# The end of a softmax attention core: the last batch's context and output product go to two free PSUM banks, and the last two batches' row numbers are worked out on VectorE

## The reference

```python
x = x + 0.5 * ffn_block(layernorm(x))
x = x + linear_attention(layernorm(x))
x = x + 0.5 * ffn_block(layernorm(x))

def ffn_block(x):
    h = layernorm(x, ln1_scale, ln1_shift)
    x = x + softmax_attention(h)            # 16 heads of 8, causal; ctx @ wo + bo
    h = layernorm(x, ln2_scale, ln2_shift)
    return x + moe(h)                       # 8 experts, the best 2 by h @ gate_w
```

## Time and profile before

| what | value |
|---|---|
| time, median of 3 runs | 1330.87 us (1326.74 to 1331.21) |
| the profiled execution's own time | 1331.67 us |
| its span, first to last instruction | 1329.9 us |
| mean granted TensorE clock | 0.890 of full speed |
| busy share PE / DVE / ACT / POOL | 76% / 81% / 58% / 41% |
| scatters to `xs` (L1385) | 128, busy 166.8 us in all |
| `back_rstd`, first instruction (L1411) | 32, mean 1373 ns, 232 to 1560 ns |

### The profile page before, as it was taken

How to read it: one execution, slowest core, us unless ns; L and a number is a source line. 1 busy time by engine, 2 the same in 40 slices (tenths; PEclk the granted TensorE clock), 3 DMA queues, 4 the chain that set the end, 5 groups by cost and what they waited for, 6 DMA issues and landing times.

```text
span 1329.9 us, 33572 instructions
## 1 busy us (share of the span) xinstructions
PE 1012.5 (76%) x11497; PEld 753.1 (57%) x11644; DVE 1077.7 (81%) x2383; ACT 771.4 (58%) x1170; POOL 549.9 (41%) x787
## 2 busy tenths in 40 slices
PE   2789888888826998367788858998898888369980
PEld 1567666666624666245455546676676666246660
DVE  5889999999965887687588768899999998458875
ACT  1369787777724555133555534687777787245550
POOL 3402456555663666210033240034465456536660
PEclk9889999999957999566888879999999999579995
DMA  3574233225202332233222206111111010023326
GB/s 101 180 233 126 83 114 112 92 78 159 62 19 73 90 89 65 89 118 116 69 64 65 62 3 202 55 40 36 40 48 44 28 50 18 21 72 88 89 65 197
DMA packets 146339, 111.57 MB, mean 84 GB/s; under 512 B 15664, under 2 KB 140848, under 8 KB 146224
## 3 DMA queue, kind: packets, MB, share of 16 engines
q1 hardware_dynamic: 124080, 78.70, 20.4%
q0 software_dynamic: 9088, 18.76, 4.0%
q10 hardware_dynamic: 13056, 12.59, 2.7%
HBM read 43.49 MB, written 59.82 MB: 78 GB/s over the span
## 4 chain that ended last, share of the span: by engine, by line
DVE 36%; issue 21%; PE 18%; ACT 11%; POOL 8%; DMA 3%; DVEq 1%; ACTq 1%; SPq 1%; POOLq 0%
DVE negm L1031 7%; POOL ys L1434 4%; DVE negm L1035 3%; DVE p_lo L1274 3%; PE banks L422 2%; ACT pf L848 2%; DVE pf L1281 2%; DVE p_lo L1043 2%; DVE x_all L989 2%; ACT p_hi L718 2%; PE banks L457 2%; PE banks L437 1%; ACT yb L741 1%; PE banks L444 1%; DVE p_lo L1047 1%
## 5 line engine op out<-in xcount | busy, mean ns | idle before, releaser
L701 ACT ACTIVATE pf<-banks 128x1536 f32<-128x1536 f32 x128 | 185.8, 1451 | 112.8 <-PE banks L444 110.0
L1043 DVE TENSOR_TENSOR p_lo<-pf,p_hi 128x1536 f16<-128x1536 f32 x128 | 223.9, 1750 | 2.9 <-ACT p_hi L718 1.9
L1434 POOL DMA_INDIRECT ys<-y_out,dest x156 | 151.6, 972 | 115.8 <-ACT y_out L854 90.8
L718 ACT CAST p_hi<-pf 128x1536 f16<-128x1536 f32 x128 | 188.7, 1474 | 2.0
L1385 POOL DMA_INDIRECT xs<-n_all,slot x128 | 166.8, 1303 | 54.9 <-issue 37.6
L1411 POOL TENSOR_SCALAR rs<-mv 128x2 f32<-128x2 f32 x32 | 43.9, 1373 | 334.3 <-DVE mv L1096 278.1
L1031 DVE TENSOR_REDUCE negm<-banks 128x4 f16<-128x1024 f32 x128 | 156.0, 1219 | 18.2 <-PE banks L422 8.9
L444 PEld LDWEIGHTS banks<-ident,negm 128*128 128x128 f16 x1536 | 122.1, 100 | 82.6 <-issue 10.0
L437 PE MATMUL banks<-qst,kst 96*128 96x512 f16 x384 | 151.5, 395 | 2.5 <-ACT pf L701 2.5
L444 PE MATMUL banks<-ident,negm 128*128 128x128 f16 x1536 | 153.1, 223 | 0.3 <-issue 0.2
L422 PE MATMUL banks<-kst,qst 96*128 96x128 f16 x1536 | 129.8, 221 | 30.6 <-DVE negm L1031 20.2
(11 more groups left out here) (197 smaller groups left out, 2471.0 us busy)
## 6 DMA issues: line engine op xcount, KB each, us to landing
xs<-zeros SPq DMA_DIRECT2D x128, 130.0 KB
qk_d<-p_hi ACTq DMA_DIRECT2D x48, 256.0 KB, 2.2
x_nats<-xs SPq DMA_DIRECT2D x78, 130.0 KB
qst<-qk_d SPq DMA_DIRECT2D x192, 48.0 KB
kst<-qk_d SPq DMA_DIRECT2D x48, 192.0 KB
pf<-ys SPq DMA_DIRECT2D x32, 256.0 KB, 3.1
v_hl<-v_all SPq DMA_DIRECT2D x48, 136.0 KB
qk_d<-p_lo SPq DMA_DIRECT2D x96, 64.0 KB, 1.7
```

The source lines that it names most:

```text
L701: nc.scalar.activation(pf[:, g % 2, :, :, :].rearrange(flat), banks_t[:, :, :].rearrange("p a b -> p (a b)"), ACT.Exp, scale=HD ** -0.5).t ...
L718: nc.scalar.copy(p_hi[:, g % 2, :, :, :].rearrange(flat), pf[:, g % 2, :, :, :].rearrange(flat))\
L1043: nc.vector.tensor_tensor(lo, pf[:, g % 2, :, :, :].rearrange(flat), hi, ALU.subtract)\
L1434: nc.gpsimd.indirect_dma_start(ys, bass.IndirectOffsetOnAxis(ap=dest[:, t % YB, h:h + 1], axis=0), y_out[:, t % YB, h, :], None).then_inc( ...
```

## The change

It rearranges the code behind the loop in the two softmax cores, for batches 14 and 15.

- Batch 15's context turn and output product no longer use `mx`. They go to `psum[0]` and `psum[1]`, two of the three banks of natural scores, whose last use is the scores of batch 15's last group. A semaphore `last_ctx` orders the four steps (`last_turn`, `last_turned`, `last_wo`, `back_add`). The bias is put in ahead, in `last_bias`.
- The order of the uses of `mx` is then: rank of 13, h2, gate and rank of 14, h2, gate and rank of 15.
- PE: `last_turn` stands before `back_h2` of 14, `last_wo` before its `back_gate`.
- ACT: `y_hat` and `pv_read` of 15 stand before `n2_norm` of 14, `last_turned` behind it. A wait for `n2_kept` stands before `n2_norm` of 15.
- DVE: the low part of batch 15's last group stands before `place_of` of 13 and `x_step` of 14; `back_add` of 15 before `choose` of 14.
- The row numbers of batches 14 and 15 are made on DVE (a new `slots` there), right behind `place_of`. POOL makes them for the batches up to 13.
- POOL: the last scatter of batch 12 stands before `back_rstd` of 14, and `back_rstd` of 15 before the last scatter of 13.
- `split_low(2)` moves behind the tables of the first expert stage.

```diff
         def fill_no(ph, b, name):
...
-            if name == "rank" and isinstance(b, int) and b == B - 1:
-                return 5 * b + 4
+            if isinstance(b, int) and b >= B - 2 and name not in ("b1", "b3"):
+                return {(B - 2, "b6"): 0, (B - 2, "b8"): 1, (B - 2, "rank"): 2, (B - 1, "b6"): 3, (B - 1, "b8"): 4,
+                        (B - 1, "rank"): 5}[b, name] + 5 * B - 8
...
+            def last_turn(ph):
+                pe.wait_ge(ph["cx_in"], ph["n"] * B + B)
+                for t in range(T):
+                    ins = nc.tensor.transpose(psum[0][:, t * P:(t + 1) * P], cx[:, t, :], ident[:, :])
+                ins.then_inc(last_ctx, 1)
+            def last_bias():
+                nc.tensor.matmul(psum[1][:, 0:T * P], ident[:, :], bo_b[:, :].unsqueeze(1).to_broadcast([P, T, P]),
+                                 start=True, stop=False, skip_group_check=True)
+            def last_wo(ph):
+                pe.wait_ge(last_ctx, of_last(ph, 2))
+                for t in range(T):
+                    ins = nc.tensor.matmul(psum[1][:, t * P:(t + 1) * P], cxt[:, t * P:(t + 1) * P], w_o[ph["w"]][:, :],
+                                           start=False, stop=True, skip_group_check=True)
+                ins.then_inc(last_ctx, 1)
...
                 if ph["soft"]:
                     back_rank(ph, B - 3)
-                    back_h2(ph, B - 2)
-                    back_gate(ph, B - 2)
+                    last_bias()
...
                 values(ph, B - 1, S - 1, at(0))
-                back_turn(ph, B - 1)
-                back_wo(ph, B - 1)
+                if ph["soft"]:
+                    last_turn(ph)
+                    back_h2(ph, B - 2)
+                    last_wo(ph)
+                    back_gate(ph, B - 2)
...
+            def last_turned(ph):
+                sc.wait_ge(last_ctx, of_last(ph, 1))
+                nc.scalar.copy(cxt[:, :], psum[0][:, 0:T * P]).then_inc(last_ctx, 1)
...
                 p_high(ph, B - 1, S - 1)
                 if ph["soft"]:
+                    y_hat(ph, B - 1)
+                pv_read(ph, B - 1, 1)
+                if ph["soft"]:
                     n2_norm(ph, B - 2)
-                    y_hat(ph, B - 1)
+                    last_turned(ph)
                     h2_turned(ph, B - 2)
                     gates_out(ph, B - 2)
                     keep_n2(ph, B - 2)
-                pv_read(ph, B - 1, 1)
-                ctx_turned(ph, B - 1)
                 if ph["soft"]:
+                    sc.wait_ge(ph["n2_kept"], B - 1)
                     n2_norm(ph, B - 1)
...
+            def slots(ph, b):
+                c = Chain(ve, ph["cp_slot"], b * 5)
+                ve.wait_ge(ph["cp_slot"], 5 * b)
+                c.link(nc.vector.tensor_tensor(at_slot[:, :, :, :], onehot2[:, b, :, :, :],
+                                               pos[:, b, :, :].unsqueeze(2).to_broadcast([P, T, 2, E]), ALU.mult))
+                for w in (4, 2, 1):
+                    c.link(nc.vector.tensor_tensor(at_slot[:, :, :, 0:w], at_slot[:, :, :, 0:w],
+                                                   at_slot[:, :, :, w:2 * w], ALU.add))
+                nc.vector.tensor_copy(slot[:, T * b:T * (b + 1), :], at_slot[:, :, :, 0]).then_inc(ph["cp_slot"], 1)
...
                 back_add(ph, B - 2)
                 if ph["soft"]:
+                    p_low(ph, B - 1, S - 1)
                     place_of(ph, B - 3)
                     x_step(ph, B - 2)
-                    p_low(ph, B - 1, S - 1)
-                    choose(ph, B - 2)
                 back_context(ph, B - 1)
                 if ph is phases[0]:
                     split_low(0)
                 back_add(ph, B - 1)
                 if ph["soft"]:
+                    choose(ph, B - 2)
                     place_of(ph, B - 2)
+                    slots(ph, B - 2)
                     x_step(ph, B - 1)
                     if ph is phases[0]:
                         split_low(1)
                     choose(ph, B - 1)
-                    if ph is phases[0]:
-                        split_low(2)
                     place_of(ph, B - 1)
+                    slots(ph, B - 1)
...
                 tables()
+                if m is mixtures[0]:
+                    split_low(2)
                 full(0)
...
+                    scatter(ph, B - 4, 3)
                     back_rstd(ph, B - 2)
-                    scatter(ph, B - 4, 3)
                     slots(ph, B - 3)
-                    for n in range(4):
+                    for n in range(3):
                         scatter(ph, B - 3, n)
                     back_rstd(ph, B - 1)
-                    slots(ph, B - 2)
+                    scatter(ph, B - 3, 3)
                     for n in range(4):
                         scatter(ph, B - 2, n)
-                    slots(ph, B - 1)
                     for n in range(4):
                         scatter(ph, B - 1, n)
```

More of the change, by code:

```diff
@@ L235, in build @@
                        **sems(n, of_soft if soft else of_linear)) for n, soft in enumerate((True, False, True))]
-        e_in = sem("e_in")
+        e_in, last_ctx = sem("e_in"), sem("last_ctx")
         mixtures = [dict(**sems(f"m{n}", "x_turn x_hi_in h2f_in x_lo_in up_done silu_in hid_in hid_hi_in hid_lo_in down_done "
@@ L265, in at_loop, with of_last @@
             return lambda d: ((4 + n + d) % RB, i + (4 + n + d) // RB)
+        def of_last(ph, n):
+            return ph["n"] // 2 * 4 + n
         def fill_no(ph, b, name):
@@ L544, in attention @@
                 values(ph, B - 1, S - 1, at(0))
-                back_turn(ph, B - 1)
-                back_wo(ph, B - 1)
+                if ph["soft"]:
[3 more added lines that the diff above has]
+                    back_gate(ph, B - 2)
+                else:
+                    back_turn(ph, B - 1)
+                    back_wo(ph, B - 1)
                 if ph["soft"]:
@@ L826, in attention @@
                     keep_n2(ph, B - 2)
-                pv_read(ph, B - 1, 1)
-                ctx_turned(ph, B - 1)
+                else:
+                    ctx_turned(ph, B - 1)
                 if ph["soft"]:
+                    sc.wait_ge(ph["n2_kept"], B - 1)
                     n2_norm(ph, B - 1)
@@ L1068, in back_add @@
             def back_add(ph, b):
-                ve.wait_ge(ph["filled"], fill_no(ph, b, "b3") + 1)
-                src = mx[:, 0:T * P].rearrange("p (t d) -> p t d", t=T)
+                last = ph["soft"] and isinstance(b, int) and b == B - 1
+                if last:
+                    ve.wait_ge(last_ctx, of_last(ph, 3))
+                else:
+                    ve.wait_ge(ph["filled"], fill_no(ph, b, "b3") + 1)
+                src = (psum[1] if last else mx)[:, 0:T * P].rearrange("p (t d) -> p t d", t=T)
                 c = Chain(ve, ph["cv_back"], b * ph["back_links"])
@@ L1089, in back_add @@
                     ve.wait_ge(ph["n2_in"], b)
-                nc.vector.tensor_tensor(y2[:, :, :], src, yb[:, :, :], ALU.add).then_inc(ph["emptied"], 1)
-                ve.wait_ge(ph["emptied"], fill_no(ph, b, "b3") + 1)
+                ins = nc.vector.tensor_tensor(y2[:, :, :], src, yb[:, :, :], ALU.add)
+                if last:
+                    ins.then_inc(last_ctx, 1)
+                    ve.wait_ge(last_ctx, of_last(ph, 4))
+                else:
+                    ins.then_inc(ph["emptied"], 1)
+                    ve.wait_ge(ph["emptied"], fill_no(ph, b, "b3") + 1)
                 for t in range(T):
```

## The result

The changed kernel takes 1308.72 us (median of 6 runs, 1306.4 to 1313.6), the kernel before 1326.78 beside it (6 runs, 1323.56 to 1331.21): a ratio of 0.9864 with an interval of 0.9838 to 0.9889. The forecast was 1315, its range 1309 to 1322: the direction is right, and the time lies 0.3 us under the range. The profiled execution took 1313.6 us, 18.07 less than the one of before (1331.67), with a span of 1311.5.

What follows compares the result with a forecast made beforehand. Each softmax core's last scatter was taken to open the expert stage, so its delay bounds the kernel. 1331.67 - 8.4 (first core) - 7.7 (second) = 1315.6, or 1314.8 from the median; stated as 1315 us, range 1309 to 1322.

Steps and rivals of the forecast that it cites:

- Rival 3: Both ends: batches 14 and 15 still run one after the other; 1329 to 1331 us, no change; chance 0.05.
- rival 2: Both ends: dearer handovers and `slots` at its upper bound, so only part is kept; 1320 us; chance 0.17.
- Rival 4: Expert stages: TensorE's clock stays at 1.2 GHz for longer, cancelling the gain or reaching 1339 us; chance 0.04.
- batch 15's statistics: Both ends: they reach POOL 8.1 us behind the start, at 376.6 in the first core and 1144.1 in the second.
- the third pass: First core, behind the tables: ends at 396.2, costing nothing while the 2.3 us before the first tile last.
- The first weight pass: First core, DVE from 372.5 to 374.8: holds batch 13's first scatter on POOL to 375.65.
- The second weight pass: First core, DVE from 380.45 to 382.75: holds the scatter behind batch 15's root to 383.6.
- signs that the prediction gave for being wrong: Root of 15 waits for something besides POOL's queue, POOL waits for `slot` in the first core, or first tile for DVE.
- the first core's term: First softmax core's end: last scatter issued at 392.85 in place of 401.26, 8.4 us sooner.
- the second's: Second softmax core's end: last scatter issued at 1157.8 in place of 1165.48, 7.7 us sooner.
- the base of the sum: Whole kernel: the profiled execution's 1331.67 us, from which the gains were taken, 0.8 above the median of the runs.
- rival 1: First core: scatters slip past the weight passes, so batch 15's numbers set the end; some 3 us more, 1312; chance 0.14.

Runs made afterwards that it cites:

- passes_moved: The changed kernel with the first weight pass ahead of `back_add` of 14 and the second where the first stood: 1305.44 us, 0.9832 against the kernel before.
- fill_for_passes: The changed kernel with the first two weight passes replaced by fills of zero, leaving out the low parts of `w1` and `w2`: 1304.69 us, one execution.
- slots_pool: The changed kernel with the row numbers of batches 14 and 15 made on POOL again: 1317.1 us, 0.9921 against the kernel before.
- numbers_of_three: `passes_moved` with the first core's row numbers of batch 13 also made on DVE: 1313.7 us, 0.9889 against the kernel before.
- slots_alone: The kernel before with only row numbers of 14 and 15 on DVE, POOL's new order and the third pass behind the tables: 1318.82 us, 0.9927.

## Why the prediction was right, and where not

**What holds.** The last scatter sets each end, its coming sooner is worth its microseconds once per core, and the two ends gave 7.5 and 8.0 us for 8.4 and 7.7. Rival 3 falls: the batches interleave. So does rival 2: `slots` on DVE took from 389.42 to 390.43, 1.0 us for 1.1, and from the end of batch 15's root to its numbers were 7.2 us (383.27 to 390.43), as foreseen (380.0 to 387.2). Rival 4 falls: the two expert stages together took 267.42 us before and 266.77 after, at clocks of 0.95 and 0.96, and 266.6 to 267.7 in the other profiles.

Step by step in the first core, counted from POOL's start: batch 14's root was held by the low part (1.53) as forecast; batch 15's statistics were done 8.1 us behind (377.32), which with the 0.2 us to POOL makes 8.3 for 8.1; the third pass ended at 399.08, 1.0 us before the first tile was in (397.87 + 2.23 = 400.10), where 2.3 were forecast. In the second core the root of 15 began at 8.69 (8.67 foreseen) and the numbers let POOL go on at 17.62 (17.9).

**Terms that were off.** All times from POOL's start at 368.50 or 369.26. *The first weight pass* was to hold the first scatter of 13, to 7.15. It held the cast ahead of it instead (2.12 us), and the scatter after that ended at 7.75. The root behind it on POOL was put off by the same 0.6: it began at 10.35 for 9.7. *The second weight pass* was to hold the scatter behind the root. It came at 11.67 (foreseen 11.95), and the root's last instruction at 11.69 (foreseen 11.3), so it held that: the root was done at 14.0 for 11.5. A scatter held there would have cost POOL's queue alone; a root held there also delays batch 15's normalisation, gate and numbers. So the numbers came at 21.2 for 18.7. POOL's queue was free for them at 20.6, where 20.5 was foreseen, so the numbers came last, and not the queue, which was to be later by 1.8 us. This is one of the signs that the prediction gave for being wrong: in the first core POOL stands waiting for `slot`. The hold could have been read from before, where the second pass, right behind the residual step of 15 as in the changed kernel, held that root's third instruction (2.73); the forecast took the root at its price without a hold and had it done 0.45 us ahead of the pass. `passes_moved` and `fill_for_passes` show what it cost: with the root's instruction back at 0.19 the end loses 1.5 and 3.5 us, the latter with the other hold gone too. Together the first core's term was 0.9 too large, the second's 0.3 too small; the sum of 16.1 compares with 15.6 in the profile. So this wrong step did not carry the time out of the range.

**The step that failed** is the base of the sum and its allowance. It was taken from the profiled execution, 1331.67, and checked against a median of three; the medians beside which the runs were timed were 1326.78 to 1330.22, and "the 2 us by which medians of such runs may differ" was too little. The profiled execution had a mean clock of 0.890. Of the 52 executions of this kernel beside the later runs, the 20 at 0.892 or less have a median of 1331.83 us, the 14 at 0.900 or more 1324.75: the base came from the slower of these. That the clock makes the difference is not shown by a run, only that the two go together. Of the 6.3 us between forecast and median, the base explains 4.1 (the 1330.87 known then, less 1326.78). The ends' 0.5 go the other way. The loop's 1.4 us were in no term and could not be read from the trace of before, which has one placing of the code only.

**What stays open.** With the ends' 0.5 taken off and the loop's 1.4 put on, the base leaves some 1.3 us of the miss. Put another way, ends and loop make 15.6 + 1.4 = 17.0 us, a ratio of 0.9872 on 1326.78, inside each of the three intervals of the changed kernel. The three middles are 0.986 to 0.9864, some 18.1 to 18.6 us. The 1 to 2 us between them are not settled: from batch 13's root to batch 14's differs by 4 us between profiles (15.1 at a clock of 1.00, 19.2 at 0.73), and the stretch through the linear core by 7 us between two executions of the very same changed kernel (335.51 at 0.82 and 328.44 at 0.84), so one profile of each cannot tell. Whether the change gives back some of that clock, or the executions only happened to differ, no run here separates.

**The hold, and rival 1.** Scatters that started inside a weight pass took 1.89 and 2.33 us before (379.28, and 392.73), 2.40 in `slots_pool`, 2.54 in `numbers_of_three` and 2.66 in `slots_alone`, where others take 0.97. Those that start early in a low part take 2.14 (at 361.50 before). Rival 1's reason, that scatters slip past, falls with these. In the changed kernel no scatter happened to start inside a pass, and batch 15's numbers did come last, as rival 1 had it; but the passes held the cast and the root instead, and its 3 us did not come. The Trainium skill (SBUF — State Buffer, Who interferes with whom) says that a probe did not see an instruction of this kind (`tensor_tensor`) stall a DMA, and infers why: it takes only the read interface of a shared port pair, and the making of descriptors needs the write interface. Here such a pass does hold scatters, whose row numbers lie in SBUF; by what is not shown. What the same section states of arithmetic, that a DVE instruction with two SBUF inputs contends with a GpSimd instruction that reads SBUF, agrees with the held cast and root. What it states of DVE instructions with at most one SBUF input, that outside the two-port modes they do not contend, agrees with the fill.

## What to carry to other kernels

When two batches are interleaved at an end, look at each long DVE subtraction for the POOL instruction that starts inside it: a held scatter costs a queue, a held step of the chain costs the chain, and an error of half a microsecond in the forecast decides between them. A wait of DVE ahead of the chain is a place for such a pass only as far as it lasts: a pass of 2.28 us in a wait of 1.0 gave back 1.1, though the same wait had been 2.31 in another profile. And take the base of a forecast from a median with its spread, not from the profiled execution, and look at the granted clock of the execution that you read: here it was a larger part of the miss than any term of the change.

## What the hardware showed unexpectedly

- A held POOL instruction that takes some 0.2 us by itself ends 0.05 to 0.11 us behind the pass (373.51 + 2.12 = 375.63 for a pass until 375.58), the root's third, of 0.72, some 0.6 behind (386.62 for 386.05 before), a held scatter 0.83 to 0.95 (377.20 for 376.37 in `numbers_of_three`, 387.27 for 386.32 in `slots_alone`). A fill of 0.91 us in the same place held neither a cast nor a scatter.
- A loop that no edit touched took 1.4 us more or less by what DVE code stands ahead of it: 0.11 us between two instructions, once per batch.
- The stretch through the linear core took from 328.4 to 339.6 us in profiles of kernels that do not differ there but for the padding, with the mean granted clock there going from 0.84 down to 0.80; one kernel on one core differed by 7 us from one execution to the next.
